# Where the offset and the old products stand in two accumulations of a chunked training scan

## The reference

```python
x = x + 0.5 * ffn(layernorm(x))        # 8 experts, 2 of them for each token, and one shared
x = x + attn(layernorm(x))
x = x + 0.5 * ffn(layernorm(x))

def attn(x, W_Q, W_KV, W1, b1, W2, b2):          # x: (2, 1024, 128)
    k, v = split(x @ W_KV)
    def step(params, kvt):                       # one time step, both sequences
        g = grad(mean((mlp(params, k_t) - v_t) ** 2))
        return params - 0.001 * g
    params = scan(step, (W1, b1, W2, b2), (k, v))     # 1024 steps, one after the other
    return mlp(params, x @ W_Q)                  # mlp(h) = silu(h @ W1 + b1) @ W2 + b2
```

## Time and profile before

| | us |
|---|---|
| median of 3 runs | 485.46 |
| lowest, highest | 484.73, 485.86 |
| the profiled execution's own time | 485.11 |
| its span, first to last instruction | 483.3 |
| busy: TensorE matmuls / weight loads | 430.8 / 354.9 |
| busy: VectorE / ScalarE / GpSimd | 282.0 / 244.2 / 236.9 |

### The profile page before, as it was taken

One profiled execution on the slowest core, in us unless ns is written; L12 is line 12 of the kernel. 1 busy time (PEld: TensorE's weight loads), 2 busy tenths in 40 slices (PEclk: granted clock), 3 DMA queues, 4 the chain that ended last, 5 costly groups with the idle time before them and its releaser, 6 DMA issues.

```text
span 483.3 us, 9854 instructions
## 1 busy us (share of the span) xinstructions
PE 430.8 (89%) x2877; PEld 354.9 (73%) x2877; DVE 282.0 (58%) x1045; ACT 244.2 (51%) x617; POOL 236.9 (49%) x341
## 2 busy tenths in 40 slices
PE   7999699999908989999999999989989599999940
PEld 5544499999903679999999999974644399999930
DVE  3865355555529657677677777754975245555514
ACT  3693255555510445655655556545786145555520
POOL 4167777544410344465555555642047777454530
PEclk9799999999966999999999999999899999999985
DMA  8971325100065200000000000000001417110028
GB/s 228 263 274 52 111 85 173 34 28 28 18 169 169 64 1 1 2 2 2 1 3 0 1 2 2 2 1 1 2 23 50 117 50 205 35 33 28 20 61 218
DMA packets 34514, 30.90 MB, mean 64 GB/s; under 512 B 3838, under 2 KB 30085, under 8 KB 34464
## 3 DMA queue, kind: packets, MB, share of 16 engines
q1 hardware_dynamic: 24608, 19.17, 14.7%
q0 software_dynamic: 4544, 8.47, 5.4%
q10 hardware_dynamic: 5312, 2.62, 2.1%
HBM read 15.55 MB, written 15.61 MB: 64 GB/s over the span
## 4 chain that ended last, share of the span: by engine, by line
PE 79%; DMA 6%; DVE 4%; POOL 4%; issue 3%; ACT 1%; ACTq 0%; SPq 0%; DVEq 0%; POOLq 0%
PE bank L1275 17%; PE bank L710 15%; PE bank L697 14%; PE bank L658 4%; PE bank L568 4%; DMA stage<-y_dram 3%; POOL slots_dram L1402 3%; PE bank L668 2%; PE bank L1069 2%; PE bank L685 2%; PE bank L1144 2%; PE bank L587 2%; DMA stage<-slots_dram 2%; PE bank L1107 1%; PE bank L1129 1%
## 5 line engine op out<-in xcount | busy, mean ns | idle before, releaser
L1656 DVE TENSOR_TENSOR sq<-bank,relu 128x512 f32<-128x512 f32 x86 | 59.4, 691 | 89.2 <-ACT relu L810 88.9
L1407 POOL DMA_INDIRECT y_dram<-y_out,stage x78 | 76.7, 983 | 59.7 <-ACT y_out L836 52.5
L1402 POOL DMA_INDIRECT slots_dram<-rows,slots x64 | 63.4, 991 | 55.5 <-ACT rows L761 27.2
L710 PE MATMUL bank<-proj_w,sq 128*128 x624 | 86.5, 282 | 2.8 <-DVE sq L1656 2.8
L697 PE MATMUL bank<-tileT,tile_w 128*128 128x128 f32 x624 | 83.1, 277 | 0.0
L710 PEld LDWEIGHTS bank<-proj_w,sq 128*128 128x128 f32 x624 | 75.7, 191 | 6.5 <-issue 3.8
L810 ACT ACTIVATE relu<-bank 128x512 f32<-128x512 f32 x94 | 56.0, 595 | 46.4 <-PE bank L697 37.6
L697 PEld LDWEIGHTS bank<-tileT,tile_w 128*128 128x128 f32 x624 | 76.9, 194 | 0.0
L836 ACT ACTIVATE y_out<-bank,stage 128x128 f32<-128x128 f32 x78 | 28.6, 367 | 33.5 <-PE bank L710 33.5
L1270 POOL TENSOR_TENSOR sq<-sq,last_rows 128x128 f32<-128x128 f32 x32 | 14.6, 456 | 53.0 <-DVE sq L1246 53.0
L568 PE MATMUL bank<-ones 128*128 128x512 f32 x34 | 22.2, 801 | 15.5 <-DVE res L1707 12.6
(11 more groups left out here) (268 smaller groups left out, 1020.5 us busy)
## 6 DMA issues: line engine op xcount, KB each, us to landing
slots_dram<-pad SPq DMA_DIRECT2D x2, 2535.0 KB, 13.8
stage<-slots_dram SPq DMA_DIRECT2D x18, 260.0 KB, 5.1
fc_w<-experts SPq DMA_DIRECT2D x1, 2048.0 KB, 20.5
proj_w<-experts SPq DMA_DIRECT2D x1, 2048.0 KB, 24.1
stage<-y_dram SPq DMA_DIRECT2D x8, 256.0 KB, 5.5
stage<-y_dram ACTq DMA_DIRECT2D x8, 256.0 KB, 6.2
y_dram<-y_out,stage POOLq DMA_INDIRECT x78, 2.3
res<-x SPq DMA_DIRECT2D x4, 256.0 KB, 3.9
```

Source lines behind the costliest of these rows:

```text
L710: last = nc.tensor.matmul(bank[4 + i % 2][:, 0:P], sq[:, i % 2, f_cols], proj_w[:, k, f_cols], start=j == 0, stop=j == FJ - 1)
L1402: nc.gpsimd.indirect_dma_start(to, bass.IndirectOffsetOnAxis(slots[:, n:n + 1], 0), rows[:, k, b, :], None, bounds_check=limit, oob_is_err ...
L1407: nc.gpsimd.indirect_dma_start(y_dram.ap(), bass.IndirectOffsetOnAxis(tiles[:, t, P:P + 1].bitcast(U32), 0), y_out[:, t % YBUFS, :], None, ...
L1656: nc.vector.tensor_tensor(wide_of(i)[2], wide_of(i)[0][:], wide_of(i)[1], ALU.mult)\
```

## The change

The order of the two accumulations of the chain ahead is turned round. In t_bank the joined product `pe_yrows` opens (start=True), behind it come the offset, now with 128 columns, and the old product, and the last of them counts yrows_done. In d_bank `pe_da` opens, behind it comes the old product with 128 columns (only the gradient's half), and it counts da_done. The zero columns are gone from w2_ident and guess_rows, and two memsets of them from GpSimd's list at the program's start. ScalarE's copy into guess_rows is now one contiguous block of 256 columns. No instruction of TensorE is added or taken away.

```diff
         def pe_offset(pe, step, turn):
 
             x = step.chain
             pe.wait_ge(offset_done, 2 * step.block + (1 if x is ahead else 2))
             if x is ahead:
-                if step.n:
-                    pe.wait_ge(x.erows_done, step.n)
-                wait_param(pe, step, turn, "w2")
-                nc.tensor.matmul(x.t_bank[:, 0:2 * P], x.offset, ident_zero, start=True, stop=False)
+                ins = mm(x.t_bank, x.offset, ident_r, start=False, stop=step.old is None)
+                if step.old is None:
+                    ins.then_inc(x.yrows_done, 1)
...
         def pe_old_guess(pe, step):
...
-            mm(x.t_bank if x is ahead else x.d_bank, old.chain.aa[:, old.to, :], old.chain.ed[:, old.to, 0, :],
-               start=False, stop=False)
+            ins = mm(x.t_bank if x is ahead else x.d_bank, old.chain.aa[:, old.to, :], old.chain.ed[:, old.to, 0, :],
+                     start=False, stop=x is ahead)
+            if x is ahead:
+                ins.then_inc(x.yrows_done, 1)
...
         def pe_yrows(pe, step, turn):
...
             if x is ahead:
-                nc.tensor.matmul(x.t_bank[:, 0:2 * P], x.a, w2_ident[:, 0:2 * P], start=False, stop=True)\
-                  .then_inc(x.yrows_done, 1)
+                if step.n:
+                    pe.wait_ge(x.erows_done, step.n)
+                nc.tensor.matmul(x.t_bank[:, 0:2 * P], x.a, w2_ident[:], start=True, stop=False)
...
         def pe_da_old(pe, step):
...
             if x is ahead:
-                pe.wait_ge(x.guess_done, step.n + 1)
-                pe.wait_ge(x.d_done, step.n)
-                nc.tensor.matmul(x.d_bank[:, 0:2 * P], x.ee[:, old.to, :], zero_rows, start=True, stop=False)
+                mm(x.d_bank[:, P:2 * P], x.ee[:, old.to, :], x.rows[:, 0:P], start=False).then_inc(x.da_done, 1)
                 return
...
         def pe_da(pe, step):
...
             if x is ahead:
-                nc.tensor.matmul(x.d_bank[:, 0:2 * P], x.e, e_w2t[:], start=step.old is None, stop=True)\
-                  .then_inc(x.da_done, 1)
+                if step.n:
+                    pe.wait_ge(x.d_done, step.n)
+                ins = nc.tensor.matmul(x.d_bank[:, 0:2 * P], x.e, e_w2t[:], start=True, stop=step.old is None)
+                if step.old is None:
+                    ins.then_inc(x.da_done, 1)
...
-            nc.gpsimd.memset(guess_rows[:, P:2 * P].bitcast(F32), 0.0)
-            nc.gpsimd.memset(w2_ident[:, 2 * P:3 * P].bitcast(F32), 0.0)
...
                 pe_first(pe, late[1], turn)
                 if early:
-                    pe_offset(pe, early[0], turn)
                     pe_aa(pe, early[0], turn)
                 pe_inner(pe, late[0])
                 if early:
                     pe_y(pe, early[0], turn)
                     pe_yrows(pe, early[0], turn)
+                    pe_offset(pe, early[0], turn)
                 pe_da_old(pe, late[0])
...
                 if early:
+                    pe_aa(pe, early[1], turn)
+                pe_da_old(pe, late[1])
+                if early:
+                    pe_yrows(pe, early[1], turn)
                     pe_offset(pe, early[1], turn)
-                    pe_aa(pe, early[1], turn)
                     pe_old_guess(pe, early[1])
-                pe_da_old(pe, late[1])
-                if early:
-                    pe_yrows(pe, early[1], turn)
                     pe_y(pe, early[1], turn)
                 pe_da(pe, late[1])
...
                 if early:
-                    pe_da_old(pe, early[1])
                     pe_inner(pe, early[1])
...
                 if early:
                     pe_da(pe, early[1])
+                    pe_da_old(pe, early[1])
                 pe_w2t_sums(pe, late[1], upd2_done)
```

More of the change, by code:

```diff
@@ L243, in mk_macaron @@
         ahead_a, ahead_w1 = (sb(n, [P, P], F32R) for n in ("ahead_a", "ahead_w1"))
-        w2_ident = sb("w2_ident", [P, 3 * P], F32R)
-        ahead_w2, ident_r, ident_zero = w2_ident[:, 0:P], w2_ident[:, P:2 * P], w2_ident[:, P:3 * P]
+        w2_ident = sb("w2_ident", [P, 2 * P], F32R)
+        ahead_w2, ident_r = w2_ident[:, 0:P], w2_ident[:, P:2 * P]
         e_w2t = sb("e_w2t", [P, 2 * P], F32R)
         ahead_e, ahead_w2t = e_w2t[:, 0:P], e_w2t[:, P:2 * P]
-        guess_rows = sb("guess_rows", [P, 3 * P + 2], F32R)
-        ahead_guess, zero_rows, ahead_rows = guess_rows[:, 0:P], guess_rows[:, P:3 * P], guess_rows[:, 2 * P:3 * P + 2]
+        guess_rows = sb("guess_rows", [P, 2 * P + 2], F32R)
+        ahead_guess, ahead_rows = guess_rows[:, 0:P], guess_rows[:, P:2 * P + 2]
         ahead_aa, ahead_ee = (sb(n, [P, 3, P], F32R) for n in ("ahead_aa", "ahead_ee"))
@@ L1206, in act_guess_rows @@
             act.wait_ge(x.yrows_done, step.n + 1)
-            nc.scalar.copy(guess_rows[:, 0:3 * P].rearrange("p (a d) -> p a d", d=P)[:, 0::2, :],
-                           x.t_bank[:, 0:2 * P].rearrange("p (a d) -> p a d", d=P)).then_inc(x.guess_done, 1)
+            nc.scalar.copy(guess_rows[:, 0:2 * P], x.t_bank[:, 0:2 * P]).then_inc(x.guess_done, 1)
         def act_rows(act, step):
@@ L1335, in _ @@
             nc.gpsimd.memset(rowmask[:], 0.0)
-            nc.gpsimd.memset(guess_rows[:, P:2 * P].bitcast(F32), 0.0)
-            nc.gpsimd.memset(w2_ident[:, 2 * P:3 * P].bitcast(F32), 0.0)
-            nc.gpsimd.memset(guess_rows[:, 3 * P:3 * P + 2].bitcast(F32), 1.0)
+            nc.gpsimd.memset(guess_rows[:, 2 * P:2 * P + 2].bitcast(F32), 1.0)
             nc.gpsimd.memset(last_rows[:], 1.0)
@@ L1884, in _ @@
                 pe_key_part(pe, *key_part(5 * step.n))
+                pe_yrows(pe, step, -1)
                 pe_offset(pe, step, -1)
@@ L1887, in _ @@
                     pe_old_guess(pe, step)
-                pe_yrows(pe, step, -1)
                 pe_aa(pe, step, -1)
@@ L1894, in _ @@
                 pe_key_part(pe, *key_part(5 * step.n + 2))
+                pe_da(pe, step)
                 if step.n:
                     pe_da_old(pe, step)
-                pe_da(pe, step)
                 pe_key_part(pe, *key_part(5 * step.n + 3))
@@ L1962, in _ @@
                 if early:
-                    pe_offset(pe, early[1], turn)
                     pe_aa(pe, early[1], turn)
-                    pe_old_guess(pe, early[1])
                 pe_da_old(pe, late[1])
@@ L1968, in _ @@
                     pe_yrows(pe, early[1], turn)
+                    pe_offset(pe, early[1], turn)
+                    pe_old_guess(pe, early[1])
                     pe_y(pe, early[1], turn)
```

## The result

| | runs | median us | lowest, highest |
|---|---|---|---|
| before | 9 | 485.86 | 484.73, 489.21 |
| after | 9 | 490.33 | 490.04, 493.25 |

The ratio after to before is 1.0097, 95% interval 1.0077 to 1.0118: slower, by 4.7 us. Forecast were 490.2 us and a turn of 9.62 to 9.64 us. The columns went away as the diff says, and the time went up because of where the products now stand in TensorE's queue.

What follows compares the result with a forecast made beforehand. TensorE's queue bounds in dense stretches, with waits on ScalarE and VectorE round trips between them. 15 turns x 0.34 = 5.1, less 0.3 at the start, on 485.46 gave 490.3, said as 490.2 us; range 486.8 to 491.6.

Steps and rivals of the forecast that it cites:

- What a column costs: TensorE's queue: 0.11 us per weight load from 2 to 256 columns; fewer columns only bring the result 0.06 us earlier.
- Second step ahead, t_bank, 0.22: Offset and old guess leave waits for places ahead of `pe_da` of `late[1]`, which starts two 0.11 us slots later.
- Second step ahead, d_bank, 0.12: Old error product behind `pe_da` makes `pe_w2t_sums`, b_sb and ahead_ee one slot later; turn grows 0.34 us with t_bank's 0.22.
- First step ahead, 0: Offset behind the joined product: between 0 and one 0.11 us slot, taken as 0 since a round trip sets the pace.
- Before the loop, 0: Three steps between key and value matmuls: 0 to one slot each, 0.3 us in all, taken as 0.
- ScalarE's copy, 0: ScalarE's contiguous copy reads and writes as many elements: 0.
- The start, -0.29: Two memsets leave GpSimd's list, so TensorE's first product (L1854) comes 0.29 us earlier, or 0 if input transfer is late.
- The sum: Whole kernel: 15 turns x 0.34 = 5.1, less 0.3 at the start, +4.8 us; said as 490.2.
- A (columns count): Rival: each narrower product frees TensorE's queue 0.06 us, order worth nothing; 3.0 us faster with the start, 482.5; 9%.
- B (slots taken up): Rival: sums of `late[1]` fed early or turn's end absorbs the delay; only 0.05 a turn remains, 486.0; 6%.
- C (one slot of three): Rival: `pe_da_old` of `late[1]` goes two slots earlier, so the turn grows by only 0.11 us; 486.9; 6%.
- D (first step paid): Rival: offset behind its joined product delays guess_rows and VectorE's queue, one slot more each turn, 1.7 us; 491.9; 12%.

Runs made afterwards that it cites:

- e3: After with 256 columns in all products again and the two memsets back, new order kept; ratio to before 1.0128, turn 9.70 us.
- e1: Before with only the t_bank part: offset (128 columns) and old guess behind the joined product; ratio to before 1.0084, turn 9.52 us.
- e2: Before with only the d_bank part: old error product (128 columns) behind `pe_da`; ratio to before 1.0015, turn 9.40 us.
- e7: After with joined product and offset of `early[1]` moved ahead of `pe_da_old` of `late[1]`; ratio to before 1.0044, turn 9.45 us.
- e5: Before plus one unused 128-column product each turn, ahead of `pe_aa` of `early[1]`; ratio to before 0.9994, turn 9.29 us.
- e6: Before plus one unused 128-column product each turn, behind `pe_yrows` of `early[1]`; ratio to before 1.0025, turn 9.40 us.

## Why the prediction was right

**What a column costs: right for the queue.** Spacing stayed 0.11 with 128 columns as with 256. The prediction put the shorter result (0.06) into the sum at no place that governs; measured against e3 it is worth 0.07 a turn. Both are true: 0.05 of it fall in the first step and keep that step at cost 0.

**Second step ahead, t_bank, 0.22: right.** Piece 2 grows by 0.22, in e1 alone by 0.23. Every distance named beforehand is there: 0.67 from `pe_da_old` to `pe_da`, and VectorE's last_ed and the sums 0.22 later. The idle mark at `pe_aa` is 0.31 instead of the 0.27 that was forecast; `pe_aa` itself starts as late after the turn's first load as before (5.89 and 5.88). `pe_da_old` of `late[1]` has no idle mark, but starts 0.30 behind `pe_aa`. The idle of L1116's place went to `pe_inner` (0.16 at 256.53), as one of the two ways that were named.

**Second step ahead, d_bank, 0.12: right to 0.02.** Piece 3 grows by 0.10, in e2 by 0.10. b_sb and ahead_ee are 0.33 late against `pe_da_old`, ahead_ed 0.28 (forecast 0.34, 0.34, 0.27). That the late path runs through `pe_w2t_sums` and b_sb, not through `pe_da`, fits these rows; no run took b_sb out of the path.

**First step ahead, 0: right, but closer than it looked.** Piece 1 is 6.19 against 6.18. With 256 columns it is 6.24 (e3): as soon as the result is not 0.06 shorter, 0.06 of the slot's 0.11 is paid. The reason given, that a round trip sets the pace there, holds only together with the shorter result.

**Before the loop, 0: not contradicted.** The transpose ahead of the three steps (L1873) is 1.25 later in after and the scan's first weight load, behind them, 1.18, so in these two traces the three steps cost nothing.

**ScalarE's copy, 0: right.** The copy into guess_rows takes 0.37 us in before (L1207), in after and in e3.

**The start, -0.29: open.** The prediction calls L1854 TensorE's first product; it is not, products on a matrix of ones stand ahead of it. The two memsets are gone and the first of these starts at 2.65 instead of 2.94. At the next load that matters, the one of the earlier trace rows, the timeline of after has

```profile
6.23 0.50 PEld L1854 LDWEIGHTS bank<-router_sb,ones 128*128 128x128 f32 x2 [1.37 <-POOL rowmask L1370]
...
6.86 0.17 DVE L1714 SCALAR_TENSOR_TENSOR router_c<-bank,router_sb 128x8 f32<-128x8 f32 x1 [6.86 <-PE bank L1854]
```

0.06 earlier for the load, 0.13 for VectorE's operation behind it (6.99 in before). In e7, which has the same start, the load comes at 6.07 and that operation at 6.70. But e2 has both memsets and its operation comes at 6.72, so this one moves by as much without the change. The load stands at 6.29 to 6.31 in the seven kernels with the memsets and at 6.03 to 6.23 in the three without: 0.06 to 0.28 earlier. In after the sign that was named, everything 0.29 earlier right after the start, holds for the first product and not for this load. What of it is left at the end can't be told: the scan's first load lies between 177.83 and 179.47 in kernels with the same start.

**The sum.** 15 turns x 0.33 = 5.0, less 0 to 0.29; timed 4.5 (difference of the medians) to 4.7 (ratio), forecast 4.7. That the median of 490.33 meets the 490.2 to 0.1 is in part luck: the median of before is 485.86 with 9 runs, not the 485.46 from which the forecast starts. Of the rivals, A (columns count) is refuted by e3's spacing and by after's 9.63; B (slots taken up) by e1, where neither of its two slots was taken up; C (one slot of three) by pieces 2 and 3; D (first step paid) by piece 1; with wide columns about half of its slot is paid (e3).

## What to carry to other kernels

On an in-order engine an instruction is priced by its place: in a wait it was free here (e5), in a dense stretch it cost its slot of 0.11 us (e6) and delayed the next round trip with it. So before products are moved to save columns or zeros, list the engine's waits and see whether the products stand in one; and look for work that can be put into each wait that is left, which here gave 0.6% with no instruction removed. Don't read the duration of a pipelined matmul as its cost: the distance to the next start is the cost in the queue, the duration counts only for whoever waits for the result.

## What the runs showed of the hardware

- An accumulated fp32r product takes 0.11 us of TensorE's queue with 128 and with 256 columns, as do single fp32 passes with 2; but the result of 256 columns comes 0.06 later (364 against 304 ns in the earlier trace rows, 0.55 against 0.49 in e3 and after).
- The duration of a matmul's row depends on its neighbours: the offset with 128 columns shows 225 ns behind the joined product, and the one of the other chain with as many columns and other neighbours 306 in the same kernel. This was not expected, and it misleads whoever sums durations.
- The granted clock fell to a mean of 0.86 in 178 to 190 us of the profiled execution of after, between the two levels, and that first turn took 11.78 us. e3's took 11.85 in its profiled execution, also at 0.86. In before the same stretch had 1.00 and 10.04 us, though TensorE had been idle for 1.25 us just ahead of it in both. The other seven kernels had first turns of 9.84 to 10.27. The steady turns alone give the 490.3 of most of after's runs, so those can hardly contain the fall. 3 of the 9, at 492.75 to 493.25, lie 2.4 to 2.9 higher, more than the 1.7 of that turn; whether they all contain it can't be told from their times, since before's runs spread by 4.5 too. Whether the new order makes it likelier, and what decides it, stays open: each kernel has one profile.
